# Sixteen residual tile loads of a fused attention and FFN kernel, given out by ScalarE in place of SyncE

## The chip, the cores and the metric

The kernel runs on one core of one Trainium2 chip. The metric is device time in microseconds (us) of one execution. Most executions agree closely: the three timed ones of the kernel before lie between 1874.05 and 1874.95 us.

## The reference

One gated cross-attention layer and one gated sparse FFN, in float32, over 32 batches of 64 tokens with 512 features (2048 tokens):

```
x = x + tanh(g_xattn) * attn(layernorm(x), ctx, mask, bias)    # 32 heads of 128
x = x + tanh(g_ffn)   * ffn(layernorm(x))

attn: q = ln(x) @ Wq;  k, v = ctx @ Wk, ctx @ Wv               # Wq, Wk, Wv: 512 x 4096
      p = softmax(q k / sqrt(128) + bias, masked);  out = (p v) @ Wo
ffn:  inter = x @ c1.T @ c2.T                                  # rank 16, 1792 columns
      one winner (argmax) in each block of 32 columns; h = relu(w1[winner] . x);  out = h @ w2t[winner]
```

## The kernel before, in words

Every float32 matrix is held as a high and a low part, and each product of the large matrices is three matmuls (lines 1439 to 1441). The tokens are 16 tiles of 128 rows; a half is 8 tiles.

**Three stages.** The first forms k, v and q, weight unit by weight unit, and stores them to DRAM (to about 960 us of the span). The second is attention. The third is the FFN, tile by tile, from about 1500 us on.

**Attention** runs in 128 slots. There are 16 rounds (`it`) of 8 slots (`p`): 8 rounds for the 8 tiles of the first half, each with 4 heads, then 8 for the second half. A slot multiplies scores, normalizes them, applies them to v and projects the result with Wo into PSUM. VectorE adds this onto `attn_sum` of the tile (`add_wo`, line 1230; the addition is L1244). In the **last round of a half** (slots 56 to 63, and 120 to 127) the tile's sum is complete. `add_wo` then also does L1248: `attn_sum * gate + x_tile`, which waits for the tile's original x. Those x tiles come in through two buffers (`xres`, called `x_tile` in the profile). The load of tile t (`load_x`) may start when L1248 of tile t-2 has ended, which the semaphore `dve_acc` counts. The result is x1; SyncE stores it to DRAM (`store_x1`, L569), and the FFN reads it back (`load_x2`, L579) into other buffers, whose profile name is also `x_tile`.

**Order is written by hand**, one program for each engine; engines meet only through semaphores. Two slots make a duo d:

- SyncE (SP) gives out every DMA of the kernel. Its attention loop goes over slots: the store of an x1 tile of four slots before, a weight piece (L534), the next round's `v` (p = 2), `kt` (p = 4), `qt` (p = 6) and `bias_in` (p = 7), then `load_x`, then stores of split FFN weights (L539). Near the end it also issues the loads of split FFN weights w1 (L546, one pair at each of slots 120 to 126) and `load_x2` of tile 3 at slot 125.
- ScalarE (ACT), for duo d: `chi` (the high part of the attention output, L884, two instructions), `probs_t` of d+1 (L874), `exps` of the two slots of d+2 (L863, 8 ACTIVATEs), then in some duos `hi_piece` (L934), `fx_hi` (L941) or `sel` (L950).
- VectorE (DVE), for duo d: `add_wo` of the slot 2d-3, low parts of the attention output (L1227), score bias and row maximum (L1137, L1142) and normalization (L1147, L1149) of duo d+2, with `add_wo` of slot 2d-2 between them.
- TensorE (PE), for duo d: attend (L1542), in every other duo scores (L1506), transposes of probabilities (L1522), and `project_out` of slots 2d-2 and 2d-1.
- GpSimd (POOL): bias plus mask, and low parts of weight pieces (L753).

At the passage to the FFN, VectorE takes the layernorm statistics of tiles 2 and 3 (L1050), finds block maxima (L1291) and their first places (L1299 to L1310), and picks h (L1320). TensorE's transposes of it (L1663) wait for these.

Of the kernel before, what the change touches and what calls it, by code (L numbers as in the profile page):

```python
# [20 lines left out]
PPH = PAIRS // HALVES  # L21
# [33 lines left out]
G = 8  # L55
HG = 4
SCORE_BANK, PT_BANK, PV_BANK, WO_BANK = (7, 0), (3, 2), (4, 5), (1, 6)
ITERS = HALVES * G
SLOTS = ITERS * PPH
DUOS = SLOTS // 2  # L60
# [61 lines left out]
def build(nc, x, ctx_t, bias, mask, gates, wq, wk, wv, wo, c1, c2, w1, w2, out):  # L122
# [18 lines left out]
    with ExitStack() as whole:  # L141
# [4 lines left out]
        def at(name, shape, dt, kb):  # L146
            return nc.alloc_sbuf_tensor_at(name, shape, dt, offset=base + int(kb * 1024))

        def sem(name):
            return whole.enter_context(nc.semaphore(name))  # L150
# [66 lines left out]
        xres = [at(f"x_tile{i}", [P, D], F32, 172 + 2 * i) for i in range(2)]  # L217
# [68 lines left out]
        xres_in = [sem(f"dma_x{i}") for i in range(2)]  # L286
# [16 lines left out]
        dve_acc = sem("dve_acc")  # L303
# [60 lines left out]
        def job_raw(r):  # L364
            _, is_v, i = JOBS[r]
            return vraw[i % 2] if is_v else kraw[i % 2]

        def job_dest(r):
            _, is_v, i = JOBS[r]
            return vw[i // 8][i % 2] if is_v else kw[i % 2]  # L370
# [72 lines left out]
        def _(sp):  # L443
# [50 lines left out]
            def load_kt(it):  # L494
                if it == 0:
                    for c in o_out:
                        for i in range(2):
                            sp.wait_ge(o_out[c][i], stored(78 + i))
                    sp.wait_ge(pe_p[3], 80)
                elif it == 1:  # L500
                    sp.wait_ge(pe_p[3], NU)
                else:
                    sp.wait_ge(pe_score, PPH // 2 * (it - 1))
                if it == G:
                    for c in o_out:
                        for i in range(2):
                            sp.wait_ge(o_out[c][i], stored(NU - 2 + i))
                sp.dma_start(kt[it % 2][:, :, :], k_d[it].rearrange("p h a t -> p h (a t)"))\
                    .then_inc(kt_in[it % 2], 16)

            def load_qt(it):
                sp.dma_start(qt[it % 2][:, :, :], q_d[it].rearrange("p h a t -> p h (a t)"))\
                    .then_inc(qt_in[it % 2], 16)

            def load_bias(it):
                if it >= 2:
                    sp.wait_ge(dve_s, PPH * (it - 1))
                sp.dma_start(bias_in[it % 2][:, :, :], bias[it]).then_inc(bias_sem[it % 2], 16)

            def load_v(it):  # L520
                if it >= 2:
                    sp.wait_ge(pe_pv, PPH * (it - 1))
                sp.dma_start(v[it % 2][:, :, :, :], v_d[it].rearrange("q t i e -> q t (i e)"))\
                    .then_inc(v_in[it % 2], 16)

            def load_piece(n):
                kind, i, cols = PIECES[n][:3]
                if n >= 2:
                    sp.wait_ge(*split_done(n - 2))
                elif n == 0:  # L530
                    sp.wait_ge(pool_wo0, 2)
                else:
                    sp.wait_ge(pe_p[3], NU)
                sp.dma_start(raw[n % 2][:, 0:cols], source(kind, i)).then_inc(raw_in[n % 2], 16)  # L534

            def store_kept(i):
                sp.wait_ge(*split_done(piece_no[("kept", i)]))
                for k in range(2):
                    sp.dma_start(kept_d[i, k], kept[k][:, :].bitcast(F32)).then_inc(kept_out, 16)  # L539

            def load_w1(n):
                if n == 0:
                    sp.wait_ge(pe_pv, SLOTS - PPH)
                    sp.wait_ge(dve_s, SLOTS - PPH)
                for k in range(2):
                    sp.dma_start(w1s[k][:, n * PIECE:(n + 1) * PIECE].bitcast(F32), kept_d[n, k])\  # L546
                        .then_inc(w1_in[n], 16)
# [11 lines left out]
                for k in range(2):  # L559
                    sp.dma_start(w2s[n][k][:, :].bitcast(F32), kept_d[W1_PIECES + n, k]).then_inc(w2_in[n], 16)  # L560

            def load_x(t):
                if t >= 2:
                    sp.wait_ge(dve_acc, t - 1)
                sp.dma_start(xres[t % 2][:, :], x[t]).then_inc(xres_in[t % 2], 16)

            def store_x1(t):
                sp.wait_ge(dve_acc, t + 1)
                sp.dma_start(x1_d[t], acc[:, t % PPH, :]).then_inc(x1_out[t % PPH], 16)  # L569

            def load_x2(t):
                if t >= X2R:
                    sp.wait_ge(out_sem[t % X2R], 16 * (t // X2R))
                elif t == 3:
                    sp.wait_ge(dve_s, SLOTS)
                elif t == 4:
                    sp.wait_ge(pe_wo, SLOTS - PPH)
                sp.wait_ge(x1_out[t % PPH], 16 * (t // PPH + 1))
                sp.dma_start(x2[t % X2R][:, :], x1_d[t]).then_inc(x2_in[t % X2R], 16)  # L579
# [7 lines left out]
            for n in range(NU):  # L587
# [13 lines left out]
                t, late = divmod(n - LN_AT + 1, 2)  # L601
# [4 lines left out]
                t, late = divmod(n - LN_AT - 2, 2)  # L606
# [32 lines left out]
            for s in range(SLOTS + 5):  # L639
                it, p = divmod(s, PPH)  # L640
                if 4 <= s:
                    it4, p4 = divmod(s - 4, PPH)
                    if it4 % G == G - 1 and it4 < ITERS:
                        store_x1(PPH * (it4 // G) + p4)
                for n in range(NP):
                    lead = {"wo": 4, "kept": 3}.get(PIECES[n][0], 1)
                    if n < 2 and s == 0 or n >= 2 and PIECES[n][3] - lead == s:
                        load_piece(n)
                if s == 0:
                    load_kt(1)  # L650
                    load_qt(1)
                if s == 1:
                    load_bias(1)
                if p == 2 and it + 1 < ITERS:
                    load_v(it + 1)
                if it + 2 < ITERS:
                    if p == 4:
                        load_kt(it + 2)
                    if p == 6:
                        load_qt(it + 2)  # L660
                    if p == 7:
                        load_bias(it + 2)
                if it % G == G - 1 and it < ITERS:
                    load_x(PPH * (it // G) + p)
                for n in range(NP):
                    if PIECES[n][0] == "kept" and PIECES[n][3] + 2 == s:
                        store_kept(PIECES[n][1])
                if SLOTS - 8 <= s < SLOTS - 8 + W1_PIECES:
                    load_w1(s - SLOTS + 8)
                if s == SLOTS - 14:  # L670
                    sp.wait_ge(kept_out, 32 * KEPT)
                    for t in range(3):
                        load_x2(t)
                if s == SLOTS - 3:
                    load_x2(3)
                if s == SLOTS + 1:
                    load_x2(4)
# [135 lines left out]
        def _(act):  # L813
# [46 lines left out]
            def exps(s):  # L860
                act.wait_ge(dve_max, s + 1)
                for h in range(HG):
                    e = act.activation(sc[s % 2][:, h, :], sc[s % 2][:, h, :], ACT.Exp,  # L863
                                       bias=negmax[s % 2][:, h:h + 1], scale=1.0,
                                       accum_out=rsum[s % 2][:, h:h + 1])
                e.then_inc(act_exp, 1)
# [34 lines left out]
            for n in range(NU):  # L901
# [16 lines left out]
                t, late = divmod(n - LN_AT, 2)  # L918
# [34 lines left out]
            def ht_hi(t, k):  # L953
                a, w = TGRP[k]
                act.wait_ge(pe_ht, 4 * t + k + 1)
                if t:
                    act.wait_ge(pe_ou, 4 * (t - 1) + k + 1)
                act.activation(hmt[0][:, a:a + w, :].rearrange("p a b -> p (a b)"),
                               bank[f_bank[("ht", t, k)]][:, 0:w * P], ACT.Copy).then_inc(act_h, 1)

            exps(1)
            probs_t(0)
            for d in range(DUOS + 3):
                if d == 0:
                    exps(2)
                if d < DUOS:
                    chi(d, 0)
                    chi(d, 1)
                if d == 0:
                    exps(3)  # L970
                if d + 1 < DUOS:
                    probs_t(d + 1)
                if d + 2 < DUOS:
                    exps(2 * d + 4)
                    exps(2 * d + 5)
                if d == DUOS - 2:
                    fx_hi(0)
                    fx_hi(1)
                if d == DUOS - 1:
                    for k in range(4):  # L980
                        sel(0, k)
                for n in range(NP):
                    if PIECES[n][3] // 2 == d and PIECES[n][4] == "act":
                        hi_piece(n)
                if d == DUOS + 1:
                    for k in range(4):
                        sel(1, k)
# [805 lines left out]
```

## Time and profile before

| | |
|---|---|
| timed runs, median of 3 | 1874.61 us (1874.05 to 1874.95) |
| the profiled execution's own time | 1874.85 us |
| its span in the trace | 1873.0 us |
| busy: PE, PEld, DVE, ACT, POOL | 1846.8, 1591.1, 1070.9, 695.5, 966.2 us |
| granted TensorE clock, mean | 0.995 of full speed |
| PE busy, 1190 to 1260 us (around the first last round) | 68.93 us of 70 |
| PE busy, 1440 to 1530 us (second last round, passage to the FFN) | 81.92 us of 90 |

The span runs from the first to the last instruction; the execution's own time is 1.85 us longer. PE and PEld are matmuls and weight loads of the same engine, which overlap. An engine's busy time leaves out its waits, and DMA-issuing instructions are not counted as busy.

### The profile page before, as it was taken

What the parts mean: (1) busy time and instruction counts of PE and PEld (TensorE: products, weight loads), DVE (VectorE), ACT (ScalarE), POOL (GpSimd) and SP (SyncE); (2) the same over time, 40 slices, a digit from 0 to 9 for tenths busy, and PEclk for the clock granted to TensorE, in tenths of its full rate; (3) what the DMA queues carried; (4) which work ended last, traced back from release to release, by engine and by line L of the source; (5) the groups of instructions that cost most, each with busy time, mean ns of one, the idle gap of its engine ahead of it and who ended that gap; (6) DMA issues with size and microseconds to landing.
All of it is one profiled execution on the core that took longest, in us unless ns stands there. A gap on an engine that the chain in (4) does not pass through costs nothing.

```text
span 1873.0 us, 37912 instructions
## 1 busy us (share of the span) xinstructions
PE 1846.8 (99%) x15304; PEld 1591.1 (85%) x15304; DVE 1070.9 (57%) x1746; ACT 695.5 (37%) x1773; POOL 966.2 (52%) x766
## 2 busy tenths in 40 slices
PE   8999999999999999999989999999999989999999
PEld 7899988899998888888878888888888778888887
DVE  5333457333345455334356667787667787776763
ACT  4332233322333333333345556555555422222221
POOL 5867688866668888778724334343433121111110
PEclk9999999999999999999999999999999999999999
DMA  5555566644455554467658878798886640000000
GB/s 168 198 176 169 177 200 212 204 158 147 152 181 185 191 186 167 165 223 250 215 225 322 334 281 319 291 387 321 315 321 256 245 181 23 23 28 25 27 12 17
DMA packets 129693, 359.51 MB, mean 192 GB/s; under 512 B 12016, under 2 KB 53360, under 8 KB 118512
## 3 DMA queue, kind: packets, MB, share of 16 engines
q1 hardware_dynamic: 129520, 357.09, 53.2%
q8 instruction: 122, 2.00, 0.5%
q14 instruction: 51, 0.42, 0.1%
HBM read 229.11 MB, written 127.93 MB: 191 GB/s over the span
## 4 chain that ended last, share of the span: by engine, by line
PE 75%; DVE 3%; DMA 1%; issue 1%; ACT 1%; SPq 0%; DVEq 0%
PE bank L1439 21%; PE bank L1441 21%; PE bank L1440 21%; PE bank L1542 3%; PE bank L1506 3%; PE bank L1522 2%; PE bank L1663 1%; PE bank L1640 1%; DVE attn_sum L1248 0%; DMA x_tile<-in_x 0%; DMA x_tile<-x 0%; ACT scores L863 0%; DVE attn_sum L1244 0%; PE bank L1619 0%; DVE attn_t_lo L1227 0%
## 5 line engine op out<-in xcount | busy, mean ns | idle before, releaser
L1439 PE MATMUL bank<-tokens_hi,wkq_hi 128*128 128x512 f32 x888 | 347.6, 391 | 4.8 <-DVE tokens_lo L1043 2.3
L725 POOL TENSOR_TENSOR wkq_lo<-raw_wkq,wkq_hi 128x768 fp32r<-128x768 f32 x126 | 284.1, 2274 | 126.1 <-ACT wkq_hi L827 125.8
L1440 PE MATMUL bank<-tokens_lo,wkq_hi 128*128 128x512 f32 x888 | 346.4, 390 | 0.0
L1441 PE MATMUL bank<-tokens_hi,wkq_lo 128*128 128x512 f32 x888 | 346.2, 390 | 0.0
L1439 PE MATMUL bank<-wv_s_hi,tokens_hi 128*128 128x256 f32 x896 | 254.2, 284 | 0.0
L1441 PE MATMUL bank<-wv_s_hi,tokens_lo 128*128 128x256 f32 x896 | 253.5, 283 | 0.0
L1440 PE MATMUL bank<-wv_s_lo,tokens_hi 128*128 128x256 f32 x896 | 253.5, 283 | 0.0
L1439 PE MATMUL bank<-wo_hi,attn_t_hi 128*128 128x512 f32 x512 | 206.0, 402 | 2.3 <-DVE attn_t_lo L1227 2.3
L1439 PEld LDWEIGHTS bank<-tokens_hi,wkq_hi 128*128 128x128 f32 x888 | 167.2, 188 | 41.1 <-issue 3.8
L1441 PE MATMUL bank<-wo_hi,attn_t_lo 128*128 128x512 f32 x512 | 199.9, 390 | 0.0
L1440 PE MATMUL bank<-wo_lo,attn_t_hi 128*128 128x512 f32 x512 | 199.5, 390 | 0.0
L1441 PEld LDWEIGHTS bank<-tokens_hi,wkq_lo 128*128 128x128 f32 x888 | 167.1, 188 | 35.2
L1440 PEld LDWEIGHTS bank<-tokens_lo,wkq_hi 128*128 128x128 f32 x888 | 167.1, 188 | 33.9
L863 ACT ACTIVATE scores<-scores,negmax 128x64 f32<-128x64 f32 x512 | 172.2, 337 | 48.6 <-DVE negmax L1142 48.6
L725 POOL TENSOR_TENSOR wv_s_lo<-raw_wv,wv_s_hi 128x1536 fp32r<-128x1536 f32 (+1 forms) x32 | 130.1, 4065 | 89.4 <-ACT wv_s_hi L827 89.4
L1065 DVE TENSOR_TENSOR c<-bank,u 128x512 f32<-128x512 f32 x94 | 65.0, 692 | 192.8 <-PE bank L1441 192.8
L852 ACT ACTIVATE p<-bank 128x512 f32<-128x512 f32 x94 | 56.2, 598 | 316.8 <-PE bank L1441 316.8
L1439 PEld LDWEIGHTS bank<-wv_s_hi,tokens_hi 128*128 128x128 f32 x896 | 171.9, 192 | 0.3
L1440 PEld LDWEIGHTS bank<-wv_s_lo,tokens_hi 128*128 128x128 f32 x896 | 172.0, 192 | 0.2
L1441 PEld LDWEIGHTS bank<-wv_s_hi,tokens_lo 128*128 128x128 f32 x896 | 171.9, 192 | 0.0
L753 POOL TENSOR_TENSOR wo_lo<-raw,wo_hi 128x1024 fp32r<-128x1024 f32 x30 | 71.2, 2375 | 169.8 <-DVE wo_hi L1214 169.8
L1087 DVE TENSOR_TENSOR c<-bank,u 128x512 f32<-128x512 f32 x94 | 64.9, 690 | 153.7 <-PE bank L1441 153.4
(146 smaller groups left out, 3706.7 us busy)
## 6 DMA issues: line engine op xcount, KB each, us to landing
k_t<-c SPq DMA_DIRECT2D x128, 256.0 KB, 2.4
v_by_token<-c SPq DMA_DIRECT2D x128, 256.0 KB, 2.3
q_t<-c SPq DMA_DIRECT2D x128, 256.0 KB, 2.3
kt<-k_t SPq DMA_DIRECT2D x16, 2048.0 KB, 9.4
qt<-q_t SPq DMA_DIRECT2D x16, 2048.0 KB, 13.9
v<-v_by_token SPq DMA_DIRECT2D x16, 2048.0 KB, 12.3
raw_wkq<-in_wk SPq DMA_DIRECT2D x32, 512.0 KB, 4.0
raw_wv<-in_wv SPq DMA_DIRECT2D x16, 1024.0 KB, 5.5
```

The source lines that it names most:

```text
L725: pool.tensor_tensor(lo, job_raw(r)[:, a:b, :], hi.bitcast(F32), ALU.subtract)\
L753: pool.tensor_tensor(lo, raw[n % 2][:, 0:cols], hi.bitcast(F32), ALU.subtract)\
L852: act.activation(e1[n % 2][:, :], bank[n % 2][:, :], ACT.Copy).then_inc(act_e1, 1)
L863: e = act.activation(sc[s % 2][:, h, :], sc[s % 2][:, h, :], ACT.Exp, bias=negmax[s % 2][:, h:h + 1], scale=1.0, accum_out=rsum[s % 2][:, ...
L1065: dve.tensor_tensor(o_c["c12"][n % 2][:, :], bank[5 + n % 2][:, :], u2[:, :], ALU.add)\
L1087: dve.tensor_tensor(o_c["c22"][n % 2][:, :], bank[5 + n % 2][:, :], u3[:, :], ALU.add)\
L1439: pe.matmul(o, a[0], b[0], start=first_mm, stop=False, skip_group_check=not grouped)
L1440: pe.matmul(o, a[0], b[1], start=False, stop=False, skip_group_check=not grouped)
L1441: return pe.matmul(o, a[1], b[0], start=False, stop=last_mm, skip_group_check=not grouped)
L1506: mm = pe.matmul(bank[SCORE_BANK[r % 2]][h * S:(h + 1) * S, o:o + S], qt[it % 2][:, 2 * r_ + h, cols], kt[it % 2][:, 2 * r_ + h, cols], st ...
L1522: mm = pe.transpose(bank[PT_BANK[d % 2]][:, o:o + P], sc[a][:, 2 * r:2 * r + 2, :].rearrange("p h k -> p (h k)"), ident[:, :])
L1542: mm = pe.matmul(bank[PV_BANK[b]][dims, o:o + S], v[it % 2][keys, p, h, dims], pt[keys, s % 2, h, :], start=True, stop=True)
```

## The change

`load_x` moves from SyncE's program to ScalarE's, and its DMAs to ScalarE's queue. The wait on `dve_acc` and the completion semaphores stay as they were. In duo d, ScalarE issues the load of slot 2d-1 right after `chi`, ahead of `probs_t`, and the load of slot 2d after `exps`, ahead of `fx_hi`, `sel` and `hi_piece`. Only the slots of the two last rounds have a load.

```diff
@@ SyncE
-            def load_x(t):
-                if t >= 2:
-                    sp.wait_ge(dve_acc, t - 1)
-                sp.dma_start(xres[t % 2][:, :], x[t]).then_inc(xres_in[t % 2], 16)
...
-                if it % G == G - 1 and it < ITERS:
-                    load_x(PPH * (it // G) + p)
@@ ScalarE
+            def load_x(s):
+                it, p = divmod(s, PPH)
+                if it % G < G - 1:
+                    return
+                t = PPH * (it // G) + p
+                if t >= 2:
+                    act.wait_ge(dve_acc, t - 1)
+                act.dma_start(xres[t % 2][:, :], x[t]).then_inc(xres_in[t % 2], 16)
+
             exps(1)
             probs_t(0)
             for d in range(DUOS + 3):
...
                     chi(d, 1)
                 if d == 0:
                     exps(3)
+                if 0 < d <= DUOS:
+                    load_x(2 * d - 1)
                 if d + 1 < DUOS:
                     probs_t(d + 1)
                 if d + 2 < DUOS:
                     exps(2 * d + 4)
                     exps(2 * d + 5)
+                if d < DUOS:
+                    load_x(2 * d)
                 if d == DUOS - 2:
                     fx_hi(0)
                     fx_hi(1)
```

## Rows read from the trace of the kernel before

**Rows 1.** Stretches of the span: busy us of each engine, clock, DMA share, GB/s

```profile
1190.00:1260.00 70.00, 68.93 (x1009) 57.44 (x1008) 57.77 (x117) 40.27 (x170) 27.39 (x24) 1.00 0.90 350
...
1440.00:1530.00 90.00, 81.92 (x848) 67.42 (x848) 72.54 (x118) 31.91 (x102) 19.61 (x17) 0.96 0.63 232
```

**Rows 2.** VectorE, end of the first last round: start, us, instruction, [idle before]

```profile
1230.36 2.09 DVE L1248 SCALAR_TENSOR_TENSOR attn_sum<-attn_sum,gate_if_key,x_tile 128x512 f32<-128x512 f32 x1
...
1237.91 0.68 DVE L1244 TENSOR_TENSOR attn_sum<-attn_sum,bank 128x512 f32<-128x512 f32 x1
1241.43 1.26 DVE L1248 SCALAR_TENSOR_TENSOR attn_sum<-attn_sum,gate_if_key,x_tile 128x512 f32<-128x512 f32 x1 [2.84 <-DMA x_tile<-in_x]
```

**Rows 3.** SyncE's issues, 1224 to 1233 us

```profile
1224.12 0.33 SPq L565 DMA_DIRECT2D x_tile<-in_x  x1
...
1225.12 0.54 SPq L512 DMA_DIRECT2D qt<-q_t  x1
...
1230.47 0.45 SPq L518 DMA_DIRECT2D bias_in<-in_bias  x1
1232.48 0.33 SPq L565 DMA_DIRECT2D x_tile<-in_x  x1
```

**Rows 4.** Landing of the bias load of 1230.47 us, then of the x load of 1232.48 us

```profile
DMA to landing us min/median/max: 10.3/10.3/10.3
...
DMA to landing us min/median/max: 8.9/8.9/8.9
```

**Rows 5.** All sixteen x loads: the issue's ns (min/median/max), then time to landing

```profile
L565 SPq DMA_DIRECT2D x_tile<-in_x x16: 327/333/1126, 1190.6 to 1492.9; - x16
...
DMA to landing us min/median/max: 2.6/5.9/11.3
```

**Rows 6.** ScalarE in duo 32 and after, first last round

```profile
1231.10 0.60 ACT L874 ACTIVATE probs_t<-bank 128x512 f32<-128x512 f32 x1 [0.85 <-PE bank L1522]
1233.87 0.35 ACT L863 ACTIVATE scores<-scores,negmax 128x64 f32<-128x64 f32 x1 [2.18 <-DVE negmax L1142]
```

**Rows 7.** ScalarE in the second last round, duos 61 and 62

```profile
1474.22 0.83 ACT L934 ACTIVATE c_stacked<-raw 128x768 fp32r<-128x768 f32 x1
1474.95 0.61 ACT L934 ACTIVATE c_hi<-raw 128x512 fp32r<-128x512 f32 x1
1475.47 1.06 ACT L884 ACTIVATE attn_t_hi<-bank 128x512 fp32r<-128x512 f32 x2
...
1482.29 1.08 ACT L941 ACTIVATE xft_hi<-bank 128x512 fp32r<-128x512 f32 x2 [5.29 <-PE bank L1619]
```

**Rows 8.** VectorE, second last round

```profile
1474.32 0.75 DVE L1248 SCALAR_TENSOR_TENSOR attn_sum<-attn_sum,gate_if_key,x_tile 128x512 f32<-128x512 f32 x1
...
1475.54 1.01 DVE L1221 SCALAR_TENSOR_TENSOR c_stacked<-c_stacked,rows_less_hi,raw 128x768 fp32r<-128x768 f32 x1
...
1480.15 0.75 DVE L1248 SCALAR_TENSOR_TENSOR attn_sum<-attn_sum,gate_if_key,x_tile 128x512 f32<-128x512 f32 x1
1482.92 1.29 DVE L1268 TENSOR_TENSOR xft_lo<-bank,xft_hi 128x512 fp32r<-128x512 f32 x2 [2.02 <-ACT xft_hi L941]
...
1490.95 0.69 DVE L1244 TENSOR_TENSOR attn_sum<-attn_sum,bank 128x512 f32<-128x512 f32 x1 [1.84 <-PE bank L1441]
...
1494.23 0.69 DVE L1050 BATCH_NORM_STATS2 ln_stats<-x_tile 128x6 f32<-128x512 f32 x1 [0.57 <-DMA x_tile<-x]
```

**Rows 9.** SyncE's issues, second last round: an x load, then `load_x2` of tile 3

```profile
1485.69 0.33 SPq L565 DMA_DIRECT2D x_tile<-in_x  x1
...
1487.16 0.48 SPq L579 DMA_DIRECT2D x_tile<-x  x1
```

**Rows 10.** TensorE's waits, 1460 to 1530 us: total, times, longest

```profile
PE bank L1663 <- DVE h_picked_t_lo L1329: 4.4, 2, 3.0
PE bank L1663 <- DVE xft_lo L1268: 1.4, 1, 1.4
```

**Rows 11.** A stretch of 2 us of the passage, all engines and the clock

```profile
1516.00:1518.00 2.00, 1.12 (x4) 0.72 (x4) 2.00 (x3) 0.60 (x1) 0.00 (x0) 0.50 1.03 420
```

## The prediction, on record before the result

> **What bounds the kernel now.** I read the shares of each engine first: TensorE is busy 1846.8 of 1873.0 us, so nothing that leaves TensorE's idle time and clock alone can move the end. Then I took busy time by stretch. The change touches only the last round of each half of attention, and there the stretches differ. Around the first last round TensorE is idle 70 - 68.93 = 1.07 us; around the second and the passage to the FFN it is idle 90 - 81.92 = 8.08 us, with a mean clock of 0.96 [rows 1]. These 9.15 us, and the clock, are all that the change can reach for gain.
>
> Next, who ends these idle times. In the first last round VectorE is the late one: the chain of waits runs along it, and its one wait for data there is 2.84 us for the x tile of slot 63 [rows 2]. TensorE notices only 1.07 us of it. The other 1.77 us were spare time of TensorE's next input. In the passage TensorE waits 4.4 + 1.4 us for VectorE's work of picking h [rows 10]. VectorE, before that work, waits 0.57 us for the x1 tile 3 that `load_x2` reads back [rows 8] (so it was ready at 1493.66); behind it VectorE stays busy almost without a gap up to the picks.
>
> Last, why these two transfers are late. SyncE issued `qt` (2 MB) at 1225.12, `bias_in` (1 MB) at 1230.47, then x of slot 63 at 1232.48 [rows 3]. The bias landed at 1230.47 + 10.3 = 1240.8 and x at 1232.48 + 8.9 = 1241.4 [rows 4]: x landed right behind it, as one queue in order would give. And `load_x2` of tile 3 went out at 1487.16, behind the x load of slot 125 at 1485.69 [rows 9], which waited for VectorE's sum of slot 123. Its own data had been in DRAM since the first half.
>
> **The change, part by part.**
>
> *Sixteen issues leave SyncE.* They cost it 16 x 0.33 = 5.3 us [rows 5] off any path. What counts is the waits that go with them. SyncE no longer waits for the sum of slot s-2 in slot s; what paces it is the store of x1 four slots before. So `qt` of the next round goes from 1225.1 to about 1220.4 (behind the sum of slot 58) and `bias_in` from 1230.5 to about 1225, behind the sum of slot 59, whose x successor was issued at 1224.12 [rows 3]. The w1 pairs of slots 122 on are likewise 3 to 7 us earlier, and `load_x2` of tile 3 moves from 1487.2 to 1480 or 1481 (behind the sum of slot 121). With the slowest x load time, 11.3 us [rows 5], it lands by 1492.3, before VectorE asks at 1493.66. So the 0.57 us go. VectorE's work behind runs 0.57 us earlier, and TensorE's waits for it [rows 10] shrink by as much: **-0.57 us**.
>
> *Sixteen issues arrive at ScalarE.* The waits are the same semaphore and count, so twelve loads can start at about the instant at which they start now. Four (slots 56, 57, 120, 121) start later, when ScalarE comes to them, at about 1202, 1206, 1464 and 1468 us, each 6 us or more ahead of its use. For slot 63 ScalarE has ended `chi` by about 1230.3 and waits for the sum of slot 61, which ends at 1230.36 + 2.09 = 1232.45 [rows 2]. So x is issued at 1232.5 as before. It has 6.1 us until VectorE wants it at 1237.91 + 0.68 = 1238.6 [rows 2]. Two things help: `bias_in` is 5 us older, and x stands in another queue. If the queues were served as one, x would still land right behind the bias, now near 1236; if not, near the 2.6 us of an undisturbed one [rows 5], at 1235. So the 2.84 us wait goes, and TensorE's share of it: **-1.07 us**. The rest, 1.77 us, becomes spare time of VectorE there.
>
> *What ScalarE's waits hold back.* The trace has no DMA issue on ScalarE. I bound it by SyncE's: 0.33 us (the lower and the median one) to 1.13 us (the slowest) [rows 5], and below by nothing, and take 0.33. In the first last round the held step is `probs_t` of the next duo: released at 1232.45, + 0.33 + 0.60 = 1233.38, and `exps` can start at 1233.87 anyway since they wait for VectorE's maximum [rows 6]. That is 0.49 us to spare, and duos 30 and 31 give the same. At 1.13 us each of the three is 0.31 us late, 0.93 us in all, under the 1.77. Cost: 0.
>
> In the second, the load of slot 122 waits until 1474.32 + 0.75 = 1475.07 [rows 8] and stands ahead of `hi_piece` of c2 and c1, `chi` and `probs_t`, which began at 1474.22 [rows 7]. They go 1475.40 - 1474.22 = 1.18 us later. VectorE's split of c2 (L1221) starts near 1476.2, 0.7 us late [rows 8]; if POOL's low part of c1 now falls upon L1248, that can take 2.09 in place of 0.75 us, as beside POOL's work in [rows 2], so 2.0 us late at most. VectorE's next idle time, 2.02 us [rows 8], takes that. The load of slot 124 waits for L1248 of 1480.15 + 0.75 = 1480.9, now 1481.6 to 1482.9, and stands ahead of `fx_hi` (1482.29) [rows 7, 8]: with the issue, 0 to 0.9 us late, and the next idle time of VectorE is 1.84 us [rows 8]. Cost: 0. With 1.13 us for an issue the same path gives 0.8 more at each of two issues: about 2.5 us late at `fx_hi`, 0.7 us left after the 1.84. Range of this part: 0 to +0.7.
>
> *Sum:* 1874.85 - 1.07 - 0.57 = 1873.2 for the profiled execution (1873.0 of span and 1.85 around it). That execution is 0.24 above the median of 1874.61, so the forecast is **1873.0**.
>
> **The rivals.**
>
> *No gain (1874.3 to 1874.7).* Both waits are replaced: x of slot 63 lands at 1238.6 + 1.77 = 1240.4 or later, or VectorE is held back elsewhere by as much. For it: the DMA engines are 90% busy in the stretch [rows 1], and x loads took up to 11.3 us [rows 5]. Against it: the bias that stood ahead leaves 5 us sooner. It decides from a landing time of 1240.4 - 1232.5 = 7.9 us; then 0 to 1.07 us are paid, and the passage alone gives at most 0.57.
>
> The Trainium skill speaks for this rival (page "DMA: Bandwidth & Descriptors", section "Issuing engines are not separate DMA queues"): DMAs of ScalarE and SyncE run on the same 16 engines and interleave, and a second issuer only saves issue time. Read strictly, that makes the change worth 0 here, since SyncE's issue time is off the path, and the time 1874.6. No row of before has two issuers, so the trace neither confirms nor denies the interleaving.
>
> *Slower (about 1877.8), by the clock.* ScalarE is held at slot 122 or 124 so long that TensorE waits before 1491, and its clock falls once more. The clock is already at half in the passage (0.50 at 1516 us) after TensorE's waits [rows 10, 11]. The mean of 0.96 over 90 us [rows 1] is 3.6 us lost, or 7.2 us at half. Another such spell costs up to 3.6 us, with 0.7 for the hold and 1.07 gained before it: 1874.6 + 3.2 = 1877.8. It decides from about 1.1 us for an issue on ScalarE. Against it: the median issue of an x load is a third of that [rows 5].
>
> *Faster by the clock (1870.4).* TensorE's waits in the passage get shorter by 0.57 us and the spell does not come. Of the 7.2 us at half about 2 are waiting; the other 5.2 would take half: -2.6, so 1873.0 - 2.6 = 1870.4. For it: the low clock begins just as the wait of 3.0 us ends. Against it: 5.2 of 5.8 us of waits remain.
>
> **How the numbers follow.** Forecast 0.58; no gain 0.23; faster by the clock 0.09; slower 0.10, of which some ends short of 1877.8. About 0.2% (3.75 us) is what a measurement of this kernel can tell from no change. The forecast and no gain lie well within it. Faster by over 0.2% means below 1870.9, so the clock rival and little else: 0.10. Slower means above 1878.4, the far end of the slow rival, or a price that I have not bounded: 0.06. Within: 0.84. The range reaches to the two clock cases without holding all of them, 1870.3 to 1876.4. The likeliest case's own range is 1872.4 to 1873.8, from the 0 to 0.7 us of ScalarE's hold.
>
> **What the profile after should show.** L1248 of slot 63 without a wait for x_tile, its x landing in under 6 us. No idle TensorE between 1236 and 1252 us. `bias_in` issued near 1225 and the x1 tile 3 near 1481, with no wait at L1050. `c2` and `c1` high parts about 1.2 us later, and VectorE's idle times ahead of L1268 and near 1491 shorter. Wrong would be: an issue on ScalarE of over 1 us; x loads on the second queue slower than on the first; a spell of low clock that is longer, shorter or elsewhere.

## The result: slower by 0.17%, and the profile after

| | before | after |
|---|---|---|
| median of 21 runs | 1874.05 us (1871.72 to 1876.57) | 1876.73 us (1875.37 to 1879.83) |
| ratio, 95% interval | | 1.0017 (1.0011 to 1.0023) |
| span of the profiled execution | 1873.0 us | 1873.8 us |

The ratio is 3.2 us, 2.1 to 4.3 by its interval; the two medians differ by 2.7. The spans of the two profiles differ by only 0.8 us, because the profile of before was slow in a part that is the same code in both. Its duo 24 of attention, ahead of the first changed slot (56, in duo 28), began at 1162.05 us, that of after at 1157.78. Twelve further profiles of kernels alike up to there have it between 1158.6 and 1160.5. So one span against another tells nothing at this size, and stretches must be compared from a common start.

The same stretches as in [rows 1], after:

```profile
1190.00:1260.00 70.00, 65.41 (x988) 54.51 (x987) 52.62 (x106) 36.15 (x149) 25.90 (x22) 0.98 0.91 346
...
1440.00:1530.00 90.00, 82.38 (x847) 67.85 (x847) 72.59 (x120) 32.49 (x104) 19.12 (x17) 0.94 0.65 236
```

TensorE is idle 4.59 us around the first last round, not 0 as forecast and not 1.07 as before. In the passage it is idle 7.62 us in place of 8.08. The loss is in the first last round. VectorE there, each L1254 (L1248 of before) that waited for its x tile, as in [rows 2]; they are those of slots 56, 59 and 61:

```profile
1206.29 0.75 DVE L1254 SCALAR_TENSOR_TENSOR attn_sum<-attn_sum,gate_if_key,x_tile 128x512 f32<-128x512 f32 x1 [0.66 <-DMA x_tile<-in_x]
...
1221.67 0.75 DVE L1254 SCALAR_TENSOR_TENSOR attn_sum<-attn_sum,gate_if_key,x_tile 128x512 f32<-128x512 f32 x1 [3.74 <-DMA x_tile<-in_x]
...
1229.66 2.34 DVE L1254 SCALAR_TENSOR_TENSOR attn_sum<-attn_sum,gate_if_key,x_tile 128x512 f32<-128x512 f32 x1 [1.10 <-DMA x_tile<-in_x]
```

The wait for slot 63 is gone, as forecast. A longer one has come at slot 59. The issues of after, at slot 59 (SyncE's, then ScalarE's):

```profile
1210.67 0.33 SPq L534 DMA_DIRECT2D raw<-in_w  x1
1211.05 0.43 SPq L508 DMA_DIRECT2D kt<-k_t  x1
...
1211.22 0.33 ACTq L961 DMA_DIRECT2D x_tile<-in_x  x1
```

And how long the two took to land:

```profile
kt<-k_t SPq DMA_DIRECT2D x1, 2048.0 KB, 10.4
...
x_tile<-in_x ACTq DMA_DIRECT2D x1, 256.0 KB, 10.4
```

Before, SyncE's own list had them the other way round, since it waited for the sum and issued x in slot 59, and kt in slot 60:

```profile
1214.95 0.33 SPq L565 DMA_DIRECT2D x_tile<-in_x  x1
...
1216.27 0.50 SPq L508 DMA_DIRECT2D kt<-k_t  x1
```

There x landed 3.1 us after its issue. After the change it goes out 0.17 us behind 2 MB of kt and takes 10.4. The chain of waits of after runs through it (start, us):

```profile
1208.91 2.30 DVE attn_sum L1254
1211.22 10.42 DMA x_tile<-in_x
1221.67 0.76 DVE attn_sum L1254
1222.45 7.18 DMA x_tile<-in_x
```

Each late sum also makes a later load late, since the load of tile t waits for the sum of tile t-2: the second link is x of slot 61. Two of TensorE's idle places that come of it, then the stretch around the longer of them (in 8 us from 1236 on the mean granted clock is 0.79, where it was 1.00 before):

```profile
1228.02 0.66 PE L1528 MATMUL bank<-ident,scores 128*128 128x128 f32 x4 [0.29 <-DVE scores L1155]
1238.14 1.12 PE L1528 MATMUL bank<-ident,scores 128*128 128x128 f32 x4 [2.85 <-DVE scores L1155]
```

```profile
1236.00:1244.00 8.00, 5.86 (x22) 4.95 (x23) 7.37 (x16) 4.61 (x21) 1.80 (x3) 0.79 1.03 393
```

**Why a queue of its own did not help x.** The packets that the 16 DMA engines took between 1214 and 1220 us, by queue (q1 is SyncE's, q10 ScalarE's): packets, MB, share of the engines' time.

```profile
q1 hardware_dynamic: 137, 1.96, 85.1%
q10 hardware_dynamic: 105, 0.22, 11.8%
```

Once both queues move, packets go one for one: 93 to 94 between 1215 and 1220 us. But one of SyncE's is 14.3 KB in the rows above (kt's rows are 16,384 bytes) and one of ScalarE's 2.1 KB (x's rows are 2,048). Taking turns by packet, x gets about a ninth of the bytes: its 128 rows need as many turns as kt's 128 rows, and it lands when kt does.

Turns set the pace, but not the start. The x tile was issued at 1211.22, and up to 1214 us its queue moved no packet, while SyncE's moved 133. No run takes this first wait apart; e4 below shows it again.

### The profile page after: what moved, and what is told of

It reads as the page before. It is cut to its first block, busy times and chain, and to the rows that moved or that the text cites. A ratio compares the mean times of both kernels' runs of the same rounds, so it can differ in the third digit from the quotient of the medians.

```text
span 1873.8 us, 37912 instructions
## 1 busy us (share of the span) xinstructions
PE 1843.4 (98%) x15304; PEld 1588.8 (85%) x15304; DVE 1071.1 (57%) x1746; ACT 696.3 (37%) x1773; POOL 965.7 (52%) x766
## 4 chain that ended last, share of the span: by engine, by line
PE 74%; DVE 2%; DMA 2%; issue 1%; ACT 0%; DVEq 0%; ACTq 0%
PE bank L1445 21%; PE bank L1447 21%; PE bank L1446 21%; PE bank L1548 3%; PE bank L1512 3%; DMA x_tile<-in_x 2%; PE bank L1528 2%; PE bank L1669 1%; PE bank L1646 1%; DVE attn_sum L1254 0%; PE bank L1625 0%; ACT scores L856 0%; DVE attn_sum L1250 0%; DVE is_max L1305 0%; DVE block_max L1297 0%
```

## The experiments

To compare profiles from a common start I take the start of TensorE's attend step (L1542 in the kernel before) of duo 24 and of duo 36, and the end of the span. Undisturbed, TensorE needs 97.88 us from the one to the other; the twelve duos from 36 on take just that in every profile. "Late" is what a profile took over that: it is the whole cost of the first last round, clock included. "Rest" is from duo 36 to the end.

| kernel | ratio to before, 95% | late, us | rest, us |
|---|---|---|---|
| before; the same again | 1 | 1.23; 1.82 | 611.9; 612.7 |
| after; the same again | 1.0017 (1.0011 to 1.0023) | 6.19; 7.22 | 612.0; 611.1 |
| e1 SyncE's waits kept | 1.0000 (0.9992 to 1.0009) | 1.08 | 614.3 |
| e2 ScalarE waits only | 1.0002 (0.9993 to 1.0011) | 2.63 | 612.9 |
| e3 kt before x, all on SyncE | 1.0005 (0.9996 to 1.0014) | 3.27 | 614.5 |
| e4 kt behind x | 1.0008 (0.9999 to 1.0017) | 5.47 | 611.4 |
| e5 kt in quarters | 1.0019 (1.0010 to 1.0028) | 5.63 | 612.6 |
| e6 all in 4 KB rows | 0.9991 (0.9982 to 0.9999) | 0.00 | 612.9 |
| e7 before, with e6's rows | 1.0000 (0.9991 to 1.0009) | 0.47 | 612.6 |
| e8 second last round only | 0.9993 (0.9984 to 1.0001) | 1.79 | 611.2 |
| e9 bias behind x | 0.9992 (0.9983 to 1.0000) | 1.66 | 613.7 |
| e10 e8 and e9 | 0.9983 (0.9974 to 0.9992) | 0.49 | 611.8 |

**First set: order, hold or queue?** My theory after the result: the order of kt and x costs the time. The rivals: ScalarE's waits hold `probs_t`; ScalarE's queue is slow in itself.

*e1.* The changed kernel with SyncE's waits put back, without their DMA:

```diff
+                if it % G == G - 1 and it < ITERS:
+                    tile = PPH * (it // G) + p
+                    if tile >= 2:
+                        sp.wait_ge(dve_acc, tile - 1)
```

> The changed kernel, with the semaphore waits of load_x put back into SyncE's list (without a DMA), so that kt, qt and bias_in go out as late as before. Order theory: the loss is kt's 2 MB, which now goes out 0.17 us ahead of the x tile of slot 59. Here x is ahead again and lands within 4 us, VectorE's 3.7 us wait is gone, TensorE is idle some 1 us between 1190 and 1260 us in place of 4.6, and the time is that of before, 1873.5 to 1875. Hold theory (ScalarE's waits ahead of probs_t cost the time): as slow as the changed kernel, 1876 to 1877.5, with VectorE or TensorE waiting for ScalarE. Queue theory (ScalarE's queue is slow in itself): x still takes 6 to 10 us to land, 1876 to 1877.5.

The loss was gone: 1.0000, clear of after's interval. x of slot 59 went out at 1213.41, kt at 1214.30, and x landed in 3.5 us. ScalarE still issued all x tiles and still waited. So neither its queue nor its waits cost the time by themselves; the release of SyncE is what brings the loss.

*e2.* The kernel before, with ScalarE waiting and issuing nothing:

```diff
+            def hold(s):
+                it, p = divmod(s, PPH)
+                t = PPH * (it // G) + p
+                if it % G == G - 1 and t >= 2:
+                    act.wait_ge(dve_acc, t - 1)
...
+                if 0 < d <= DUOS:
+                    hold(2 * d - 1)
...
+                if d < DUOS:
+                    hold(2 * d)
```

> The kernel before, with ScalarE waiting for dve_acc at the sixteen places of the changed kernel, but SyncE issuing the loads. Order theory and queue theory: 1873.5 to 1875, as before, TensorE idle about 1 us between 1190 and 1260. Hold theory: most of the loss is here, 1876 to 1877.

1.0002. The profile has 1.4 us more of "late" than before's first profile and 0.8 more than its second. One L1258 (L1248 of before) took 2.86 us, where [rows 2] have 2.09:

```profile
1227.92 2.86 DVE L1258 SCALAR_TENSOR_TENSOR attn_sum<-attn_sum,gate_if_key,x_tile 128x512 f32<-128x512 f32 x1
```

It ran beside GpSimd's subtraction of 1227.83 to 1230.23. Such a long sum, and a wait of 0.55 us for the x tile of slot 60, which this profile also has, come in kernels without the hold too, so they can't be put down to it with certainty. The hold may cost about 1 us by the profile, and up to 2 by the interval; it isn't most of the loss.

*e3.* The kernel before, with SyncE's order changed at one place, all on its one queue:

```diff
+                    if PIECES[n][:2] == ("kept", G - 1):
+                        lead = 4
...
-                    if p == 4:
+                    if p == (3 if it == G - 1 else 4):
                         load_kt(it + 2)
```

> The kernel before with SyncE's order changed at one place: the weight piece and kt of the next round (2 MB) are issued in slot 59 ahead of its x tile, and not in slot 60 behind it. ScalarE issues nothing. Order theory: x of slot 59 lands 9 to 11 us after its issue in place of 3.1, VectorE waits 3 to 4 us for it, TensorE is idle 3.5 to 5 us in the stretch, time 1876 to 1878. Hold and queue theory: no change, 1873.5 to 1875.

The mechanism came as foretold. VectorE:

```profile
1222.75 0.75 DVE L1250 SCALAR_TENSOR_TENSOR attn_sum<-attn_sum,gate_if_key,x_tile 128x512 f32<-128x512 f32 x1 [3.71 <-DMA x_tile<-in_x]
```

x took 10.1 us to land. TensorE was idle 2.96 us in the stretch, below the 3.5 to 5 expected, and the time (median 1875.66) just below what I had set; its ratio of 1.0005 can't be told from 1, nor quite from that of after. The order of these two loads alone gives the 3.7 us wait and, by this one profile, about 2 us of the 5 us of "late".

*e4.* The changed kernel, kt one slot later:

```diff
-                    if p == 4:
+                    if p == (5 if it == G - 1 else 4):
                         load_kt(it + 2)
```

> The changed kernel, with kt of the next round issued by SyncE in slot 61 (behind the x1 store of slot 57) in place of slot 60, so some 0.4 us behind the x tile of slot 59 and not 0.17 us ahead of it. Order theory: x of slot 59 lands within 5 us, VectorE's 3.7 us wait goes and most of the loss with it: 1873 to 1875, with waits of up to 1 us left for x of slot 61 behind qt. Hold and queue theory: 1876 to 1877.5.

x of slot 59 landed in 5.3 us and its wait was gone, but less of the loss went than I expected: the ratio of 1.0008 (0.9999 to 1.0017) lies half way, and its interval reaches to no loss and to the whole of it; "late" is 5.47 us. The next x was caught by the next big load. qt (2 MB, rows of 16,384 bytes), released early too, went out at 1218.33, and x of slot 61, issued at 1222.15, took 8.9 us:

```profile
1231.10 0.75 DVE L1254 SCALAR_TENSOR_TENSOR attn_sum<-attn_sum,gate_if_key,x_tile 128x512 f32<-128x512 f32 x1 [2.83 <-DMA x_tile<-in_x]
```

TensorE was idle 3.65 us, and the clock fell again (0.98 over the 70 us, as after). So the order theory is right but too narrow: it isn't one pair of loads, it is that all of SyncE's loads now run ahead of x. This profile also shows the late start again: x of slot 60 was issued at 1217.97, and between 1218 and 1221 us SyncE's queue moved 77 packets and ScalarE's none.

**Second set: first come, or taking turns?** If the engines serve what was issued first, x waits for all bytes ahead of it. If they take turns by packet, the size of SyncE's rows decides.

*e5* and *e6.* kt of round 9, then kt, qt, v and bias_in of rounds 8 and 9, by several DMAs with rows of 4,096 bytes; bytes, place and waits the same. For kt:

```diff
-                sp.dma_start(kt[it % 2][:, :, :], k_d[it].rearrange("p h a t -> p h (a t)"))\
-                    .then_inc(kt_in[it % 2], 16)
+                n = CUT.get(('kt', it), 1)
+                for i in range(n):
+                    h = slice(i * HG // n, (i + 1) * HG // n)
+                    sp.dma_start(kt[it % 2][:, h, :], k_d[it][:, h].rearrange("p h a t -> p h (a t)"))\
+                        .then_inc(kt_in[it % 2], 16)
```

> The changed kernel, with kt of round 9 (2 MB in rows of 16,384 bytes) loaded by four DMAs of one head each (rows of 4,096 bytes); bytes, place in the list and waits are the same. Turn theory: the DMA engines take one packet from SyncE's queue and one from ScalarE's in turn, and x's packets are 2,048 bytes, so beside packets of 16,384 x gets a ninth and lands when kt does (10.4 us); beside 4,096 it gets a third: x of slot 59 lands in 4 to 6 us, its 3.7 us wait on VectorE goes, that of slot 61 behind qt stays or grows to 2 to 3 us, as when kt was a slot later; time 1875 to 1876. First-come theory (x waits for all that was issued before it, whichever queue): x lands 10 us after its issue as in the changed kernel, 1876 to 1877.5.

> The same for kt, qt, v and bias_in of rounds 8 and 9: all in rows of 4,096 bytes, by four DMAs each (two for bias_in). Turn theory: every x tile of the first last round lands in 3 to 6 us, VectorE never waits over 0.5 us for one, TensorE is idle under 1 us between 1190 and 1260 us, and the time is that of the kernel before or up to 1 us under it, 1873 to 1874.3. First-come theory: as the changed kernel, 1876 to 1877.5.

In e5, x of slot 59 was issued at 1213.46, behind the first quarter of kt (1213.28), and landed at 1219.69, 6.2 us later; the other three quarters, issued 0.3 to 1.2 us behind x, landed at 1221.2 to 1224.0. The packets of 1214 to 1220 us of e5:

```profile
q1 hardware_dynamic: 443, 1.64, 79.7%
q10 hardware_dynamic: 144, 0.26, 12.2%
```

ScalarE's queue got its whole tile through in that time (144 packets: 128 rows, and 16 of 4 bytes). Here too the two go one for one once both move: 126 to 122 packets between 1217 and 1219 us, now with rows of 4,096 bytes on SyncE's side. The landing alone would fit first come as well, since the one quarter ahead of x had landed at 1218.93 and the others stood behind it. The time did not follow (1.0019, above what I expected): x of slot 61, behind the uncut qt, took 9.4 us, and VectorE waited 3.36 us for it.

With all of them cut, e6, the round is at TensorE's pace, and the kernel faster than before (0.9991):

```profile
1190.00:1260.00 70.00, 70.00 (x1129) 58.63 (x1127) 55.89 (x114) 40.45 (x163) 28.45 (x23) 1.00 0.96 369
```

VectorE's longest wait for an x tile there was 0.7 us, a little over the 0.5 expected; landings were 4.7 to 7.6 us, slower than I wrote. The x tile of slot 61 decides between the theories: it was issued at 1221.23, behind all four quarters of qt (the last at 1219.33), and landed at 1227.68, ahead of two of them (1228.71 and 1231.19). First come cannot give that; turns by packet can.

*e7.* The same cut in the kernel before, as the control.

> Control: the kernel before (SyncE issues the x tiles) with the same four or two DMAs for kt, qt, v and bias_in of rounds 8 and 9. One queue is served in order, so by both theories the x tiles land as before (slot 63 in 8 to 10 us) and the time is that of before, 1873.5 to 1875, unless small packets cost something of themselves.

1.0000. x of slot 63 landed in 8.4 us, behind the bias as ever. So the cut alone is worth nothing that can be measured (0.9991 to 1.0009), and with ScalarE's queue it takes the ratio from 1.0017 to 0.9991: it pays where two queues take turns.

*e8.* ScalarE issues the x tiles of slots 120 to 127 only (`if it < ITERS - 1: return` in its `load_x`, and SyncE's `load_x` kept for slots 56 to 63).

> Half of the change: ScalarE issues the x tiles of slots 120 to 127, SyncE still those of slots 56 to 63. The loss is all in the first last round, so this gives 1873 to 1874.5: the 0.57 us wait for the x1 tile 3 is gone, up to 1 us of waits for x tiles behind w1 is new. If the second last round had part in the loss: 1875 or more.

0.9993 (0.9984 to 1.0001): no loss in the second last round, perhaps a gain. The loss lies in the first.

**Third set: the better kernel, and how far one profile can be trusted.**

*e9.* The kernel before, bias_in of round 9 behind x of slot 63:

```diff
-                    if p == 7:
+                    if p == 7 and it != G - 1:
                         load_bias(it + 2)
                 if it % G == G - 1 and it < ITERS:
                     load_x(PPH * (it // G) + p)
+                if it == G - 1 and p == 7:
+                    load_bias(it + 2)
```

> The kernel before, SyncE issuing all x tiles, with one change of order: bias_in of round 9 (1 MB) goes out behind the x tile of slot 63 in place of ahead of it. By order in one queue, x of slot 63 then lands behind qt, in 4 to 6 us in place of 8.9; the 2.8 us wait and TensorE's 1.07 us in the round go: 1872.5 to 1874, ratio 0.9990 to 1.0000. If a late bias_in delays GpSimd enough to matter: 1875 or more.

*e10.* e8 and e9 together.

> The two gains together: SyncE's order with bias_in behind x in the first last round, and ScalarE issuing the x tiles of slots 120 to 127 only. 1871.5 to 1873, ratio 0.9985 to 0.9995, as good as or better than the all-quarters version (0.9991).

e9 gave 0.9992 (0.9983 to 1.0000). x of slot 63 landed in 5.6 us and VectorE did not wait for it. Yet "late" was 1.66 us in its profile, about as before; what made it is told below. e10 gave 0.9983 (0.9974 to 0.9992), median 1871.15 beside 1874.26 of before: faster than both kernels, and as much under the kernel before as the change was above it.

*e11* and *e12.* The two kernels profiled again.

> The kernel before, profiled once more. Relative to the start of duo 24 the start of duo 36 was 1.23 us behind TensorE's pace (99.11 in place of 97.88 us). If the wait for x of slot 63 is a fixed feature of this order, 1 to 2 us again; the part ahead of duo 24 may differ by up to 4 us.

> The changed kernel, profiled once more. Duo 36 was 6.19 us behind pace, 4.59 of it idle TensorE and the rest a spell of low clock at 1238 us. The x tile of slot 59 is again issued within 0.3 us behind kt and lands in 9 to 11 us; 4 to 6.5 us behind pace again, near 4.5 if the low clock does not come.

"Late" came out at 1.82 and 7.22 us, the second above my range. kt was issued at 1212.67 and x of slot 59 at 1212.85, again 0.2 us behind; x took 10.5 us. The swap is no accident of one run. SyncE comes to kt when GpSimd ends a weight piece, and ScalarE to x when VectorE ends a sum, each at a fixed place in the round.

## Why the prediction was wrong

I had written 1873.0 (1870.3 to 1876.4), faster or the same. Measured: 1876.73, slower by 0.17%. It lies outside the range and on the other side, though inside the 0.2% that I had called the same.

**The step that failed** is the landing time of the x tiles, in the first two parts of the change. I listed what goes out earlier once SyncE is free as `qt`, `bias_in`, the w1 pairs and `load_x2`. I left out `kt`. Then: "twelve loads can start at about the instant at which they start now", from which I took that they land as now, and I priced one x tile only, that of slot 63. Issued at the same instant is not landed at the same time. kt had stood 1.3 us behind x of slot 59; now it stood 0.17 us ahead. That x went from 3.1 to 10.4 us, with 6.7 us until its use. The term I wrote as -1.07 us was about +5: "late" rose from 1.23 and 1.82 us to 6.19 and 7.22. The tile of slot 56, which I had 6 us or more ahead of its use, missed it too: 9.6 us to land, and 0.66 us of waiting. e1, which takes away SyncE's release and nothing else, gives it back (1.08 us, ratio 1.0000).

**The queue.** I took the undisturbed 2.6 us as the end for a transfer in a queue of its own, and "right behind the bias" for the other, both as gains. For slot 63 that held (landed in 4.9 us, no wait). In general it did not: the queues take turns by packet, so x beside rows of 16,384 bytes took 10.4 us, as long as kt and as x behind kt in one queue (10.1 us in e3). The Trainium skill has this rule, and I cited another section of that page. "Queues, rings and completion order" in "DMA: Bandwidth & Descriptors" says that each DMA engine goes round the queues that have work and switches at packet boundaries. The counts of 93 to 94 packets agree with the turns. The section has a packet of typically 9 to 17 descriptors drained before the switch; here what took turns was single rows of 16,384 and 2,048 bytes. The section that I had cited says that a second issuer only saves issue time; read strictly, as I read it, it gave a change worth nothing. The first effect here was on SyncE's order, and it was a loss.

**The hold of ScalarE.** I costed it at nothing, and e2 bears this out within its interval (1.0002, up to 1.0011, which is 2 us). The issue took 0.353 us (median of 16), as assumed, not 1.13. But in the profile after, `probs_t` was held for 4.72 us at slot 61. An obvious rival is that this hold, with x late, makes the loss as large as it is; no run has late x tiles on ScalarE's queue without the hold. The profile of after speaks against it. The held `probs_t` ended at 1223.51, and TensorE's attend, which needs it, began only at 1224.55, when VectorE's `attn_t_lo` was there:

```profile
1224.55 1.16 PE L1548 MATMUL bank<-probs_t,v 64*64 64x64 f32 x64 [1.46 <-DVE attn_t_lo L1233]
```

At slot 63 the hold ended at 1232.03, and ScalarE's `exps` then still waited 0.33 us for VectorE's maximum. So VectorE, late by its waits for x, was the last in both places.

**The passage.** The direction was right. `load_x2` of tile 3 went out at 1481.85 (I had 1480 or 1481) and no wait was left at the statistics. New waits for x behind the w1 pieces came (1.8 us in all), partly into spare time. The size may have been off because I read it from one profile: VectorE waited 0.57 us there, but 1.10 to 1.75 us in the five other profiles with SyncE's `load_x` there (e2, e3, e7, e9, e11). "Rest" is 613.0 us in the mean of those six and 611.9 in the seven where SyncE was free of the second round's waits: 1.15 us, twice my 0.57. The profiles of each kind spread by 2 to 3 us, and e8's 0.9993 is 1.3 us with an interval that reaches to 1.0001, so the gain is likely but its size is not shown. (e1, which keeps SyncE's waits, stands in neither mean; it has 614.3.)

**The rivals.** "No gain" had the right mechanism, an x tile that lands late in full DMA traffic, but I tested it at the tile whose neighbours I had moved away, and gave it nothing below zero. The slower rival named the clock as the cause; the spell did come, in the first last round and not in the passage, as a consequence of the waits. It accounts for about 1.6 of the 6.19 us (the rest is 4.59 us idle). The sum is then 5 - 1.15, near 4 us by the profiles; the runs say 2.1 to 4.3. Both parts rest on few profiles each.

**What stays open.** Part of "late" in the profiles like before comes and goes. Where the x tile of slot 60, behind kt, kept VectorE waiting for 0.3 to 0.7 us (e8, e9, e11), GpSimd's low part of a weight fell on VectorE's normalization in place of a sum. In e11:

```profile
1228.16 2.37 DVE L1149 TENSOR_TENSOR scores<-scores,rowinv 128x256 f32<-128x256 f32 x1
```

```profile
1227.74 2.51 POOL L753 TENSOR_TENSOR w_lo_to_keep<-raw,w_hi_to_keep 128x1024 fp32r<-128x1024 f32 x1 [4.09 <-ACT w_hi_to_keep L934]
```

That step takes 0.42 us otherwise, and TensorE's next input hangs on it. No run takes this collision away. In e3, 7.1 us of waits for x cost TensorE less than the 5.5 us of after. The two profiles show where they part. The wait of 3.7 us at slot 59 is in both. Then after has the 1.10 us at slot 61, ahead of the normalization for which TensorE waits 2.85 us; in e3 that wait is 1.14 us. e3's second wait, at slot 63, begins behind that normalization, and its clock stays at 1.00. So most of the difference is this one place and the low clock behind it; no run separates the two. Nor does any run show what keeps an x tile from moving its first packet for some 3 us.

## What to carry to other kernels

Taking a wait out of a queue's list releases everything behind it. List every transfer that this moves, and for each short transfer with a near deadline ask what now stands ahead of it: issued 0.17 us behind kt, x took 10.4 us here, and issued 0.37 us ahead of it (e4) 5.3. The second queue here shared the engines by packets and not by bytes, so the transfer with small rows lost to the one with large rows; cut the large one's rows (e6), or keep it behind (e1). And read the size of a wait from several profiles where the whole effect is 0.1%.

## What the runs showed of the hardware

- Between SyncE's and ScalarE's queues the engines alternated by packet, whatever the packets held: 93 to 94 in 5 us of after, with rows of 16,384 and 2,048 bytes; 126 to 122 in 2 us of e5, with rows of 4,096 and 2,048.
- Beside rows of 4,096 bytes a 256 KB tile of 2,048-byte rows landed in 6.45 us and ahead of 1 MB that had been issued before it (e6, slot 61). Beside rows of 16,384 bytes it took 10.4 us (after, slot 59).
- With SyncE's queue busy, a tile on ScalarE's queue moved no packet for about 3 us after its issue (after, slot 59; e4, slot 60).
- Cutting 2 MB loads into four DMAs with rows of 4,096 bytes cost nothing measurable by itself (e7, 1.0000).
- A DMA issue on ScalarE takes 0.334 to 0.393 us (16 of them), as one on SyncE mostly does.
- Identical code ahead of duo 24 differed by up to 4.3 us between profiles (1157.78 to 1162.05).
